# Router logits made inside a soft attention, its first half routed there, and expert units interleaved with shared ones; a filler matmul in ten power steps

## The reference, cut to what matters

```python
f1: softmax attention, 16 heads of width 8
f2: h = rmsnorm(X)*norm1_w;  X = X + softmax_attention(h) @ wo        # second attention
    h2 = rmsnorm(X)*norm2_w
    logits = h2 @ router_w;  top 2 of 8 experts, softmax of the two
    moe = swiglu(h2, shared) + sum over the two chosen of w_e * swiglu(h2, expert e)
    return X + moe                                                     # d_ff = 256
f3: power attention: causal, |q.k|^2 with decays of cumulated log gates, 16 heads
f4: top 2 of 8 experts with a capacity, 7 real experts of width 512 and one that does nothing
```

## Time and profile before

| | us |
|---|---|
| three runs, median (lowest to highest) | 1183.83 (1175.76 to 1192.58) |
| the profiled execution, its time | 1178.53 |
| its span, first to last instruction | 1176.7 |
| PE busy | 1030.3 (88%) |
| DVE busy | 887.7 (75%) |
| ACT busy | 757.2 (64%) |
| POOL busy | 644.3 (55%) |
| mean granted TensorE clock | 0.906 |

### The profile page before, as it was taken

One profiled execution on the slowest core, in us unless ns is written; L12 is line 12 of the kernel. 1 busy time (PEld: TensorE's weight loads), 2 busy tenths in 40 slices (PEclk: granted clock), 3 DMA queues, 4 the chain that ended last, 5 costly groups with the idle time before them and its releaser, 6 DMA issues. The chain is left out here.

```text
span 1176.7 us, 30894 instructions
## 1 busy us (share of the span) xinstructions
PE 1030.3 (88%) x10524; PEld 615.7 (52%) x10524; DVE 887.7 (75%) x2262; ACT 757.2 (64%) x1638; POOL 644.3 (55%) x707
## 2 busy tenths in 40 slices
PE   4899998999999999885899889888989999938975
PEld 2344444444444444474699765555555566524752
DVE  3899998898898899674544767988888889874223
ACT  1688887888887778831355356757767689733314
POOL 3244444455344444156473647978877678725763
PEclk9999999999999999998899887967777699966998
DMA  5112222212222211001354331111121011132217
GB/s 125 33 47 57 56 56 56 55 52 56 56 56 55 57 43 32 13 24 55 108 149 133 101 86 30 54 51 43 48 61 30 22 47 45 46 133 68 53 61 202
DMA packets 116022, 75.23 MB, mean 64 GB/s; under 512 B 21335, under 2 KB 108064, under 8 KB 115872
## 3 DMA queue, kind: packets, MB, share of 16 engines
q1 hardware_dynamic: 109296, 60.71, 19.1%
q0 software_dynamic: 5888, 12.10, 3.6%
q10 hardware_dynamic: 688, 0.46, 0.1%
HBM read 26.75 MB, written 26.51 MB: 45 GB/s over the span
## 5 line engine op out<-in xcount | busy, mean ns | idle before, releaser
L621 DVE TENSOR_REDUCE mxsS<-scoreS 128x2 f32<-128x512 f32 x512 | 328.6, 685 | 45.7 <-PE scoreS L760 41.2
L509 ACT ACTIVATE PTS<-stS 128x512 f32<-128x512 f32 x512 | 283.5, 592 | 65.8 <-PE stS L764 65.1
L975 POOL TENSOR_TENSOR PTP<-PTP,EP 128x512 f32<-128x512 f32 x128 | 164.7, 1293 | 69.8 <-ACT PTP L1204 68.8
L760 PE MATMUL scoreS<-QK 31*128 31x256 f16 x1024 | 171.3, 280 | 33.5 <-DVE mxsS L621 14.8
L764 PE MATMUL stS<-QK 32*128 32x256 f16 x1024 | 167.9, 277 | 0.9 <-ACT PTS L509 0.9
L685 PE MATMUL pvS<-PTS,Vx 128*32 128x256 f32 x2048 | 140.3, 392 | 0.4
L1396 DVE TENSOR_SCALAR AP<-score_psP 128x768 int32<-128x768 int32 x128 | 121.7, 951 | 21.6 <-PE score_psP L1555 20.6
L1204 ACT ACTIVATE PTP<-AP,epsP 128x768 f32<-128x768 f32 x128 | 119.0, 930 | 25.0 <-DVE AP L1396 24.4
L760 PEld LDWEIGHTS scoreS<-QK 31*128 31x128 f16 x1024 | 53.7, 93 | 154.3 <-DVE mxsS L621 96.3
L382 POOL TENSOR_TENSOR rsS<-veS,halfS 128x2 f32<-128x2 f32 (+1 forms) x32 | 28.0, 874 | 190.2 <-DVE veS L589 103.7
L1216 ACT ACTIVATE EP<-decay_psP 128x512 f32<-128x512 f32 x128 | 75.9, 593 | 49.6 <-PE decay_psP L1537 47.8
(11 more groups left out here) (389 smaller groups left out, 2356.8 us busy)
## 6 DMA issues: line engine op xcount, KB each, us to landing
QK<-HLS SPq DMA_DIRECT2D x384, 32.0 KB, 1.9
QK<-HLP SPq DMA_DIRECT2D x192, 32.0 KB
gsin<-sorted SPq DMA_DIRECT2D x46, 128.0 KB
mixed<-gob SPq DMA_DIRECT2D x46, 128.0 KB, 1.9
sorted<-ggot SPq DMA_DIRECT2D x22, 256.0 KB, 2.4
expert_outputs<-tzero SPq DMA_DIRECT2D x8, 512.0 KB
cgot<-expert_outputs SPq DMA_DIRECT2D x16, 256.0 KB, 5.3
tokens<-XB SPq DMA_DIRECT2D x16, 128.0 KB, 3.1
```

The costliest lines, as they stand in the source:

```text
L509: act.activation(PT[:, n % NPT, :], st_ps[:, (NS * t + n) % 3, :], ACT.Exp, scale=SCALE).then_inc(s_exp, 1)
L621: dve.tensor_reduce(mxs[:, u // 4, :, at], score_ps[:, n % 2, :].rearrange("p (c s) -> p c s", c=TC), AX.X, ALU.max).then_inc(s_max, 1)
L760: scored = pe.matmul(score_ps[:, k, cols], QK[part, new, g, 0, rows], QK[part, new, g, 1, :], start=True, stop=True)
L975: eng.tensor_tensor(w, w, E[:, n % NE, :], ALU.mult).then_inc(s_wd if n % NU in MULT_BY_DVE else s_wp, 1)
```

## The change

**Logits in the attention.** At the start, once, `wo @ (norm2 * router)` is made (`route_tensor`, `route_vector`, `route_weight`). In steps t >= 16 the value projection and the output projection of the attention are 136 columns wide instead of 128, eight of them the router's. VectorE combines the two parts by a ratio of row norms (two operations on 128x8), ScalarE copies the first part, and GpSimd makes the ratio. The router's matmuls, the f16 halves of its weight, and the logits' and square sums' operations on DVE are gone.

**Rows on GpSimd.** `scaled_rows` makes the RMS by a square, seven adds of halves, a scale, a power and four row scalings, in one call, for blocks 0 to 6 in the attention's steps 19, 21, ..., 31 (place 1), and for block 7 at the gated layer's start. The table is zeroed by 24 DMAs on GpSimd's queue, two in each of steps 2 to 13.

**First half routed in the attention.** The choice for tiles 0 to 15 stands on DVE at (25,1), (25,3) and (25,5), its counting on TensorE at (26,0) in the bank of attention's misc. results, its ranking on DVE at (26,1), (26,2), (26,4), (26,5), and its 32 scatters on GpSimd, one in each place from (26,6) to (30,5). The transposes of batch 28 wait for DVE to have read the counts.

**Units interleaved.** 4 shared units, 23 sorted of the first half, 6 shared, 23 sorted of the second half, 6 shared. The second half's choice and ranking are made on DVE at units 4 to 9, its scatters follow on GpSimd. Gathers of four blocks start in the second half's units, five blocks are gathered before the power layer, three in power steps 0 to 7, three gathers a step. The block's normalization is applied on ScalarE (before: DVE), and the guests of the power layer stand at units 46 to 61 instead of 53 to 61.

**The filler.** L1519 is issued once in each place of steps 0 to 9 (before: step 0 alone).

```diff
@@ soft_layers
@@ normalized (GpSimd)
+                used = slice(0, 1 + 2 * kind)
+                pool.tensor_tensor(rs[:, used, :], ve[:, used, :], half[:, used, :], ALU.pow).then_inc(s_y, 1)
...
                 if kind == 1:
+                    pool.tensor_tensor(ratio[:, b * TC:b * TC + TC], rs[:, 0, :], rs[:, 2, :], ALU.mult)
@@ take_out (DVE)
-                dve.tensor_tensor(xt, xt, ps, ALU.add).then_inc(free["PR"], 1)
+                dve.tensor_tensor(xt, xt, ps[:, :, 0:D], ALU.add)
+                reach(dve, free["V"], t + 1)
+                for c in range(TC):
+                    n = b * TC + c
+                    last = dve.scalar_tensor_tensor(lg[:, n, :], lg[:, n, :], ratio[:, n:n + 1], ps[:, c, D:D + NE],
+                                                    ALU.mult, ALU.add)
+                last.then_inc(free["PR"], 1)
@@ project_out (TensorE)
-                last = pe.matmul(bank("PR")[:, c * D:(c + 1) * D], ynT[:, c * P:(c + 1) * P],
+                last = pe.matmul(spaced("PR", t)[:, c, 0:D + NE * (t // NB)], ynT[:, c * P:(c + 1) * P],
                                  weights[t // NB]["wo"][:], start=True, stop=True)
@@ power_layer, decays
-                for _ in range(AGAIN if t >= NB - 2 else t == 0):
+                for _ in range(AGAIN if t >= NB - 2 else t < 10):
                     pe.matmul(decay_ps[:, n % 2, :], cstb[:, 0:P], late, start=True, stop=True)
@@ gated_layer
+MOE_RUNS = (4, 6, 6)
+    ORDER = []
+    for h, run in enumerate(MOE_RUNS):
+        begun = sum(MOE_RUNS[:h])
+        ORDER += [("shared", i) for i in range(begun, begun + run)]
+        if h < NPART:
+            ORDER += [("sorted", s) for s in range(first_group[h], first_group[h + 1])]
...
         def scaled_rows(pool, b):
-            pool.wait_ge(s_y, 2 * b + 1)
-            for c in range(TB):
-                last = pool.tensor_scalar(y[:, b * TB + c, :], XB[:, b * TB + c, :], irs[:, c:c + 1], None, ALU.mult)
-            last.then_inc(s_y, 1)
+            lk = Link(pool, s_y, ROWS_OF, b)
+            pool.wait_ge(soft.free["PR"], NB + 2 * b + 2)
+            lk(pool.tensor_tensor(square, block_of(XB, b), block_of(XB, b), ALU.mult))
+            for width in (64, 32, 16, 8, 4, 2, 1):
+                lk(pool.tensor_tensor(square[:, :, 0:width], square[:, :, 0:width], square[:, :, width:2 * width], ALU.add))
+            lk(pool.tensor_scalar(ms[:], square[:, :, 0], MS_BY, EPS_RMS, ALU.mult, ALU.add))
+            lk(pool.tensor_tensor(irs[:, b * TB:(b + 1) * TB], ms[:], half[:], ALU.pow))
+            for c in range(b * TB, b * TB + TB):
+                last = pool.tensor_scalar(y[:, c, :], XB[:, c, :], irs[:, c:c + 1], None, ALU.mult)
...
-                if n in SCORES:
-                    score(pe, SCORES[n])
-                if n in COUNTS:
-                    count(pe, COUNTS[n])
-                if n == SHARED - 1:
-                    sorted_turn(pe, 0)
-                if n >= SHARED - 1 and n + 2 < UNITS:
-                    sorted_turn(pe, n + 2 - SHARED)
+                if n + 2 < UNITS and (turned_at(n + 2) or 0) >= 2:
+                    turn(pe, turned_at(n + 2))
+                if n == COUNTING:
+                    count(pe, 1, nobody)
@@ build
-                soft.sync(sp, {2 + k: functools.partial(gated.zeroed, sp, k) for k in range(ZERO_PIECES)})
+                soft.sync(sp, {})
...
+            COUNTED = NB + 2 * MOE_PARTS[0] + 2
+            LATE = range(gated.EARLY, 8)
...
+                for k in range(ZERO_PIECES):
+                    heads[2 + k // 2, 2 + k % 2 * 2] = functools.partial(gated.zeroed, pool, k)
+                for b in range(7):
+                    heads[19 + 2 * b, 1] = head("rows", b)
+                places = [(t, u) for t in range(COUNTED, SOFT_STEPS) for u in range(8) if (t, u) >= (COUNTED, 6)]
...
+                heads.update({(COUNTED - 1, 1): head("choose", 0), (COUNTED - 1, 3): head("choose", 1),
+                              (COUNTED - 1, 5): head("choose", 2), (COUNTED, 1): head("rank", 0),
+                              (COUNTED, 2): head("rank", 1), (COUNTED, 4): head("rank", 2),
+                              (COUNTED, 5): several(head("rank", 3), head("choose", 3))})
```

762 lines of the change are left out of this document (394 added, 368 removed).

## The result

The changed kernel takes 1146.85 us (median of 4, 1145.95 to 1149.46), the one before 1183.99; the ratio is 0.9706, with a 95% interval of 0.9673 to 0.9738. The time lies in the predicted range and on the predicted side, but 37 us were gained and not 78. The profiled execution has a span of 1144.5 us at a mean clock of 0.945 (before 1176.7 at 0.906).

The account below looks back on a forecast made before the run. TensorE and VectorE together were taken to bound the attention, TensorE with one long wait the gated layer, the clock the power layer; 1178.5 + 8 (attention) − 34 (gated) − 1 (opening) − 45 (power) = 1106.5, said 1106 us; range 1086 to 1158.

Parts of the forecast that it names:

- the sum for the power steps: Power layer, steps 1 to 9: full clock with the filler, 17.9 us each, 161 against 197.4, −36.3 us.
- The first rival: Power layer: the filler in vain; steps 3 to 9 keep clock 0.74, fillers cost +5 us, kernel 1156 us; chance 13%.
- Step 10: Power layer, step 10: at full clock from its start, 24.6 → 16.2 us, −8.4.
- Step 0: Power layer, step 0: comes in at a higher clock, 17.5 us where it took 21.1, −3.6.
- The gated layer: Gated layer: the long wait and its halved clock go, 164.0 against 198.3 us, −34, bounds −38 and −22.
- The two guests' waits: Gated layer: waits of 3.42 us for `yP` and 3.83 for `lgP` mostly go, 4 left.
- The attention: Attention: terms 4.8 + 4 + 1.5 − 1 − 1 sum to +8 us, bounds −5 and +16.
- The move of the zeroing: Attention: SP loses 24 issues beside the DMAs behind the row maxima (14.4 us of wait), −1 us.
- Choosing, ranking and counting: Attention: VectorE's choosing and ranking add 4.8 us; the count on TensorE and T(28)'s wait for its reading add 1.5.
- GpSimd's pile: Attention: scatters and block 4's rows make `normalized(30)` 8 us late; +4 us at TensorE, bounds 0 and 9.
- The late table: Rival, attention and gated layer: late first-half scatters make unit 4 wait and add an attention wait; 1136 us, chance 11%.
- The slower case: Power layer, steps 1 to 13: half clock lasts throughout, +138 us, kernel 1244 us; chance 3%.

## Why the prediction was right and wrong

**The step that failed** is the sum for the power steps: "I take steps 1 to 9 at full clock: 16.2 + 8 × 0.22 = 17.9 us each, 161 against 35.0 + 162.4 = 197.4: −36.3". Measured is 187.8, −9.6. The price of the filler and the full-clock step were right: of the steps without additions, 1, 2, 4, 5 and 7 ran in 17.9 to 18.9 us, and only step 8 did not (22.0, behind the last gather). What was wrong is the sentence before it, that the filler "is to leave TensorE no gap", and with it the reading of 23.2 us a step as the clock's alone. The filler stands in TensorE's program and does not run while TensorE waits for a score bank: steps 3 to 9 had 15.2 us of idle time before and have 14.7 after. The miss of 26.8 us (187.8 for 161) is 15.7 us idle in steps 1 to 9 and, by the difference, some 11 that the half clock cost. The 15 us of idle time that I quoted from the earlier trace rows were a term of their own, made by the late blocks' gathers and additions, and I carried them at nothing. The first rival named this wait ("VectorE … may hold TensorE at the same places, filler or not"), but only as a case in which the filler is in vain too; both happened, a filler that works and gaps that stay. Without that work the steps took 165.9 us, 5 from the forecast's 161.

Step 10, "24.6 → 16.2", came at 16.6, and only because no fall reached it: in four kernels with the filler to step 9 and in one without late work and filler it was at 24.1 to 24.8. Step 0, "17.5", was 19.6: three gathers stand in it beside the last early block's additions (a gap of 3.87 us), and without the gathers it was 17.4. In all the power layer gave 19.1 of 45 us; the late work accounts for 24.1 of the 25.9 that lack (290.1 against 266.0), as the kernel without it shows.

**The gated layer**, "−34", with the opening's −1 gave 21.3. The wait of 11.95 us and the half clock behind it went as forecast, and TensorE's work was 163.0 us, 4.5 over the 158.5, with 10.2 us at half clock in it. "The two guests' waits … so most of it goes: I leave 4" failed: 7.92 us for `lgP`, by the root behind the gather, plus that fall of the clock (0.78 in 665 to 688.2). The rest is 4.4 us of waits for VectorE's `XB` at units 4 and 5, where the second half's choice stands ahead of the shared additions; I had read no row for that.

**The attention**, "+8", came at +6.5 (500.8 → 507.3), near by luck: two errors cancel. The move of the zeroing, taken at −1, is worth 9 to 12 us up to step 23 when it is undone; the 14.4 us wait that I had named beside it was mostly its doing. Choosing, ranking and counting, 4.8 + 1.5, came as forecast: steps 25 and 26 took 16.9 and 19.0 us for 14.1 and 15.5, +6.3. GpSimd's pile, "+4", was 7.97 us at the place forecast, the transposes of batch 30, and step 28 took 23.2 us for 14.1. Its arithmetic was right: 18.6 us from one normalization to the next, and GpSimd's timeline has the first end at 428.44 and the next begin at 446.52, 18.1 later. The slack of 4 that I took off was not there.

**The rivals.** The filler in vain is refuted in the changed kernel (19 us) and true on the kernel before. The late table did not happen: 32 scatters ran at 1.26 us each, but for GpSimd's other work between them, beside a VectorE that was busy for 48.8 of 64.8 us (75%; beside the first half's scatters before it was 22.8 of 41.5), and the first sorted unit did not wait for its rows. The Trainium skill's trap ("SBUF — State Buffer") on DMAs issued by GpSimd, which speaks of descriptors held up by VectorE, did not show: a scatter was 0.96 us as before, and the move of 24 DMAs to that queue was a gain. It was hardly put to the test either. It is about VectorE's two-port modes, and 40.7 of VectorE's 48.8 us there were reductions of scores in PSUM (L634, 0.68 us each); no run here shows scatters beside such a mode. The slower case did not happen.

**What stays open.** Which gap brings a fall, and when: gaps of 0.34 us (without the filler) and of 3.9 us did, others of about 1 us did not, and a fall lasted from 3.4 to 27 us with the filler in place. With this go the times of one kernel, whose executions lie 3 to 18 us apart, and a wait that is taken away in front of the power layer can be given back within it.

## What to carry to other kernels

When a slow stretch has both a low clock and idle time, price them apart: one filler took half clock in steps 1 to 9 from 114 to 38 us and left the idle time where it was (16.2 and 15.7 us). Before counting a wait as gone, look at what else stands in the same queue, on GpSimd above all: a gather that waits 20 us holds every small root behind it. And moving a transfer off the queue that carries a stage's critical DMAs can be worth far more than its number suggests (forecast at 1 us, 9 to 12 here), so read which queue the longest DMA wait is on.

## What the runs showed of the hardware

VectorE's operations on two SBUF operands waited for GpSimd's two-operand multiplication: `ynP` (128x128) took 0.29 us alone and 1.93 beside two multiplications of 1.26, ending 0.16 us behind the second; four additions took 1.13 us beside gathers and 2.68 beside a multiplication, and still 2.15 when cut to one column. In such a place an operation's width is nearly free. Its number was worth little as well (one of one column in place of four: 2.9 us, not told from zero), while having none was worth 11.0 us. It is the operation itself that is stretched, not a wait ahead of it, so the sentences ahead of the prediction that the engines meet only at semaphores, and that these alone hold an engine back, are too narrow. Operations that read PSUM (`ynP` from `misc_b`, 0.29 us in all 15) were not stretched. The Trainium skill ("SBUF — State Buffer", on the two sides of SBUF) says that the port pair shared by the two engines is an exclusive lock held for a whole instruction, and that a VectorE operation with two SBUF inputs needs it against a GpSimd operation that reads SBUF. The traces agree, 0.29 against 1.93 us; they add that GpSimd operations back to back can keep VectorE's waiting through all of them. In the changed kernel this was so in five places (1.85 to 1.96 us, and 3.06 beside three), all right behind a gather; in steps 11 to 13, without a gather ahead, the wait ended 0.15 us behind the first, as here:

```profile
912.95 3.80 POOL L991 TENSOR_TENSOR PTP<-PTP,EP 128x512 f32<-128x512 f32 x3
```

```profile
913.71 0.67 DVE L1337 TENSOR_TENSOR ynP<-farP,rcP 128x128 f32<-128x128 f32 x1
```

What decides between the two is not shown.

The 24 small gathers cost more by this than by their own time: 1.03 us each on GpSimd, which had 33 of 151.7 us idle in steps 3 to 9, and yet half a microsecond of the kernel for each (12.3 us / 24) when they are taken out.
